# Weight loads in smaller runs and one gather moved, in a GNN layer followed by a mixture of experts

## The reference

```python
def _swiglu_ffn(x, wg, wu, wd):
    return jax.nn.silu(x @ wg) * (x @ wu) @ wd

x = x + _L0_gnn_ref(_layernorm(x, axis=-1), edge_index, ...)
h = _layernorm(x, axis=-1)
for e in range(2):
    shared = shared + _swiglu_ffn(h, sWg[e], sWu[e], sWd[e])
top_w, top_i = jax.lax.top_k(jax.nn.softmax(h @ Wr), 6)
for e in range(64):
    routed = routed + _swiglu_ffn(h, Wg[e], Wu[e], Wd[e]) * gate[:, e:e + 1]
x = x + (shared + routed + h)
```

## Time and profile before

| | us |
|---|---|
| median of three runs | 765.91 (764.79 to 767.23) |
| the profiled execution | 770.06 |
| its span, first to last instruction | 768.3 |
| PE busy | 706.6 (92%) |
| ACT busy | 215.8 |
| POOL busy | 174.6 |
| load queue (q1): data, share of the DMA engines' time | 211.33 MB, 71.8% |
| gather and scatter queue (q0) | 20.56 MB, 11.5% |

### The profile page before, as it was taken

The page is one execution under the profiler, slowest core; times in us unless marked ns, Lnnn a source line. Parts: engine busy times, 40 slices in busy tenths (PEclk is TensorE's granted clock), DMA queues, the critical chain, the costliest instruction groups (busy, mean ns, idle before and its releaser), DMA issues. The chain is left out here.

```text
span 768.3 us, 17261 instructions
## 1 busy us (share of the span) xinstructions
PE 706.6 (92%) x6966; PEld 476.9 (62%) x6966; DVE 254.0 (33%) x794; ACT 215.8 (28%) x526; POOL 174.6 (23%) x157
## 2 busy tenths in 40 slices
PE   2679999889999999999999999999999978999981
PEld 2567776657776666556566666665667756777650
DVE  6965635965121442222222112122233212221000
ACT  4732412402332222212222222221222321333330
POOL 4000000011222222332223223222333223332122
PEclk9999999999999999999999999999999998999996
DMA  8915022326999999999999999999999999999941
GB/s 285 410 55 219 24 86 104 127 87 225 359 356 347 387 375 390 387 393 386 380 377 392 378 390 375 389 386 385 386 381 371 367 339 363 372 372 373 373 127 23
DMA packets 57263, 236.32 MB, mean 308 GB/s; under 512 B 6171, under 2 KB 6335, under 8 KB 40286
## 3 DMA queue, kind: packets, MB, share of 16 engines
q1 hardware_dynamic: 46004, 211.33, 71.8%
q0 software_dynamic: 10144, 20.56, 11.5%
q10 hardware_dynamic: 1034, 3.30, 1.1%
HBM read 222.32 MB, written 12.83 MB: 306 GB/s over the span
## 5 line engine op out<-in xcount | busy, mean ns | idle before, releaser
L453 POOL DMA_INDIRECT out<-ysb,idx_sb x64 | 92.6, 1447 | 260.4 <-issue 198.3
L1445 PE MATMUL ps<-ring,xT 128*64 128x256 f32 x1296 | 148.3, 380 | 0.8 <-DMA ring<-in_L_ffn_Wu 0.8
L441 POOL DMA_INDIRECT xg<-x_tab,idx_sb x64 | 71.1, 1111 | 317.4 <-DVE idx_sb L1002 223.4
L995 DVE TENSOR_REDUCE gates<-ps 128x1 f32<-128x3 f32 (+1 forms) x62 | 10.0, 162 | 344.5 <-PE ps L1353 332.3
L1445 PEld LDWEIGHTS ps<-ring,xT 128*64 128x64 f32 x1296 | 93.2, 137 | 48.2 <-issue 2.4
L660 ACT ACTIVATE ysb<-ps 64x256 f32<-64x256 f32 x64 | 24.1, 377 | 225.0 <-PE ps L1445 150.1
L1445 PE MATMUL ps<-ring,hTj 128*64 128x256 f32 x624 | 77.1, 390 | 0.0
L1445 PE MATMUL ps<-w,xT 128*64 128x256 f32 x608 | 69.9, 379 | 0.0
L963 DVE TENSOR_TENSOR onehot<-iotaAB,slotv 125x640 bf16<-125x640 f32 (+1 forms) x64 | 67.3, 1051 | 1.3 <-PE ps L1361 0.8
L1445 PEld LDWEIGHTS ps<-ring,hTj 128*64 128x64 f32 x624 | 41.9, 138 | 29.6 <-issue 12.8
L1445 PEld LDWEIGHTS ps<-w,xT 128*64 128x64 f32 x608 | 44.1, 137 | 21.7 <-issue 0.4
(11 more groups left out here) (245 smaller groups left out, 823.9 us busy)
## 6 DMA issues: line engine op xcount, KB each, us to landing
ring<-in_L_ffn_Wg SPq DMA_DIRECT2D x41, 1024.0 KB
ring<-in_L_ffn_Wu SPq DMA_DIRECT2D x40, 1024.0 KB
ring<-in_L_ffn_Wd SPq DMA_DIRECT2D x39, 1024.0 KB
w<-in_L_ffn_Wd SPq DMA_DIRECT2D x20, 1024.0 KB
w<-in_L_ffn_Wg SPq DMA_DIRECT2D x19, 1024.0 KB
w<-in_L_ffn_Wu SPq DMA_DIRECT2D x19, 1024.0 KB
ring_x<-in_L_ffn_Wu SPq DMA_DIRECT2D x5, 1024.0 KB
ring_x<-in_L_ffn_Wd SPq DMA_DIRECT2D x5, 1024.0 KB
```

What stands on the lines that cost most here:

```text
L441: g.indirect_dma_start(out=xg[j % NX][0:ROWS[j], :], out_offset=None, in_=x_tab, in_offset=bass.IndirectOffsetOnAxis(ap=idx_sb[0:ROWS[j], ...
L453: g.indirect_dma_start(out=out, out_offset=bass.IndirectOffsetOnAxis(ap=idx_sb[0:ROWS[j], j:j + 1].bitcast(u32), axis=0), in_=ysb[j % NY][ ...
L1445: last = t_.matmul(ps[h * BIG:(h + 1) * BIG, bank, 0:AW], big(k), w[:, k, h * AW:(h + 1) * AW], start=(k == 0), stop=(k == KD - 1))
```

## The change

Gate and up weights of positions 44 to 63 are no longer loaded by one DMA each but by four, one for each of the four k slices of the tile. Each of them moves 256 KB in runs of 2 KB, and all four count on the slot's semaphore; `uses` and `landed` count accordingly. On POOL gather 53 moves from behind the base's dense transfer to a place between scatter 47 and that transfer.

```diff
@@ -310,13 +310,20 @@
-        uses = [len(range(s, len(items), NR)) for s in range(NR)]
+        PARTED, PIECES = 44, 4
+
+        def pieces(i):
+            r, j = items[i]
+            return PIECES if r < 2 and j >= PARTED else 1
+
+        uses = [sum(pieces(i) for i in range(s, len(items), NR)) for s in range(NR)]
 
         def landed(r, j):
-            return 16 * (item_of[r, j] // NR + 1)
+            i = item_of[r, j]
+            return 16 * sum(pieces(a) for a in range(i % NR, i + 1, NR))
 
@@ -373,7 +380,10 @@
                 else:
-                    sp.dma_start(ring[i % NR][:], experts[r][number[j]]).then_inc(s_ring[i % NR], 16)
+                    n = KD // pieces(i)
+                    for k in range(0, KD, n):
+                        sp.dma_start(ring[i % NR][:, k:k + n, :],
+                                     experts[r][number[j]][:, k:k + n, :]).then_inc(s_ring[i % NR], 16)
 
@@ -464,13 +474,14 @@
             for j in range(E + LAG):
-                if j < E and j <= BASE_AFTER + LAG + 1:
+                if j < E and j <= BASE_AFTER + LAG:
                     gather(j)
                 if j >= LAG:
                     if BASE_AFTER + LAG + 1 < j + 1 < E:
                         gather(j + 1)
                     scatter(j - LAG)
                 if j == BASE_AFTER + LAG:
+                    gather(j + 1)
                     add_base()
```

## The result

On 20 runs of each, measured beside each other, the changed kernel took 771.86 us (766.93 to 773.44) and the kernel before 768.05: a ratio of 1.0036, with an interval of 1.0022 to 1.0051. It is slower by a third of a per cent, and the interval is all on that side (the ratio is not that of the two medians, which would be 1.0050). Its profiled span is 770.2 us against 768.3, 1.9 more. The forecast was 768.0 on a median of 765.91, a ratio of 1.0027, with a span of 769.9. Over 20 runs the kernel before has a median of 768.05, 2.1 above the three runs that the forecast stood on; so the time itself came out 3.9 us above the forecast, and it is the ratio that can be compared.

What follows compares the result with a forecast made beforehand. PE, scatter chain and loads ran within 4% of each other, the scatter chain setting the end. Scatter 57 at 720.9 plus 49.0 gave span 769.9 against 768.3; taking 2.1 more on median 765.91 gave 768.0 us, range 760.5 to 774.5.

Steps and rivals of the forecast that it cites:

- The likeliest case: Whole kernel: scatter chain gains, then loses in the tail; 768.0 us, within 766 to 770, chance 0.38.
- The price of the 2 KB runs: Load queue: 0.20 us more a matrix, 8 us over 40, so loads drain at about 747 instead of 739.
- rival 2: Load queue: 2 KB runs cost 0.28 us or more a matrix, drain at 750; 770 to 776 us, chance 0.22.
- PE at position 60: PE late in the kernel: 6.8 us of load price against 6.3 slack makes it 0.5 us late, say 1.
- The gather: POOL: gather 53 goes by 613, base keeps 616; PE's 6.18 us wait goes, PE gains at most 4.5, the end nothing.
- The base: Dense transfer after scatter 47: some 2.5 us of 19 shorter, landing at 632, scatter 48 at 633.5.
- the turn of the packets: DMA engines: queues alternate one packet for one, so a 2 KB row waits for one load packet, now 2 KB instead of 8.
- The scatter interval of 8.4: Scatters beside loads: 1.3 us off an interval of 9.7; the chain catches up with PE by position 52.
- The tail: Scatter 57 to the end of the span: 49.0 us instead of 44.6, since loads drain at 747.
- Rival 1: Scatters beside loads: whole wait in the load queue shrinks, interval about 6.4 us; 759 to 764.5 us, chance 0.30.
- Rival 3: Whole kernel: loads eat PE's gain and the scatter chain keeps its pace; no change, 766 us, chance 0.10.
- SP's 120 issues at nothing: SP: 120 more DMAs, at most 3.4 us a position against 9.4, hidden by the full queue, cost nothing.

Runs made afterwards that it cites:

- e12: The changed kernel unaltered, measured again on the chip of e9 to e11: 770.19 us, 1.0027 of the kernel before.
- e1: The kernel before with only gather 53 moved in front of the base, all loads in their old runs: 767.42 us, 0.9999.
- e2: The changed kernel with gather 53 put back behind the base, 2 KB runs kept: 770.11 us, 1.0025 of the kernel before.
- e11: The changed kernel with 4 KB runs (two transfers a matrix) and gather 53 back behind the base: 764.52 us, 0.9951 of the kernel before.
- e5: The changed kernel with 2 KB runs only for gate and up of positions 52 to 59, gather moved: 766.96 us, 0.9993 of the kernel before.
- e7: The changed kernel with two transfers a matrix in 4 KB runs instead of four in 2 KB: 764.39 us, 0.9928 of the kernel before.
- e8: The kernel before, SP issuing each weight from position 44 on only once the third matrix back has landed: 765.94 us, 0.9974.
- e3: The changed kernel loading one slice of four for gate and up of positions 61 to 63 (weights partly wrong): 763.93 us, 0.9944 of the kernel before.
- e10: e7 with its 4 KB runs from position 24 on (80 matrices): 768.28 us, 0.9997 of the kernel before.
- e9: e7 with SP issuing each weight from position 44 on only once the third matrix back has landed: 769.09 us, 1.0018 of the kernel before.
- e6: The changed kernel with 2 KB runs from position 24 on, 80 matrices instead of 40: 776.92 us, 1.0095 of the kernel before.

## Why the prediction was right, point by point

*The sign and the size.* 1.0027 was forecast and 1.0036 (1.0022 to 1.0051) measured; the span grew by 1.9 us where 1.6 was computed. The likeliest case was the one that came. That the spans agree to 0.3 us is luck in part: they are single executions, and twelve runs of one kernel lie 5 to 10 us apart.

*The price of the 2 KB runs*, 0.20 us a matrix: the last load ends 9.2 us later, 0.23 for each of 40, and 15.3 us later with 80, 0.19 each. The drain at 747 was measured at 747.2. What the DMA engines pay is more. The load queue takes 3.35 us a matrix from 656 to 716 where it took 3.14, which is 0.31 for each matrix in small runs (0.24 in e12, which moves 19.04 MB there), and the packets' durations give 0.28. That the drain moved by less fits SP's queue: in the kernel before SP waited 7.1 us between 590 and 740 for PE to free a slot, in the changed kernel not at all. The prediction had SP at a full queue only, without that slack. So its 0.20, from the pair of windows with nothing else in them, hit the drain with a price of the engines that was too low, and rival 2, from 0.28 on, had nearly the right price and the wrong drain, 750. By the prediction's own terms the price at which PE falls behind is 6.3 / 34 = 0.19 and not 0.16.

*PE at position 60* was to be 0.5 to 1 us late and is 0.8. The short waits for weights stood at 51 and 52, within the 47 to 53 that the prediction named.

*The gather.* It went by 613 in the forecast and at 613.71 in the trace, and the base kept its place (615.30). That this part gives the end nothing is shown by e1 and, from the other side, by e2 and e11. That was forecast rightly, but the step "this part alone gives PE at most 4.5 us" was too kind, and so was "it would land by about 637, and PE needs it after 640": in e1 gather 54 landed at 639.9 and PE waited 4.43 us for it and 10.27 for ACT. The prediction looked only at the loads for what is late next. The chain from the base over scatter 48, ACT's y copy and `hTj` to PE, which stood in the earlier trace rows, was nearer.

*The base.* 2.5 of 19 us less was forecast; from its issue to scatter 48 it is 17.8 us (615.30 to 633.06) against 20.1, 2.4 less. The way to it was not the one computed: between 625 and 632 the load queue moved 633 packets while the other moved 428, and not one for one, so that the near agreement in size is not a proof of the turn of the packets.

*The scatter interval of 8.4.* Right as a price, wrong as a forecast of what the changed kernel would show: its intervals from 48 on are 10.75, 9.50, 9.30, 9.52, 9.47. The prediction let the chain catch up with PE by position 52; it had caught up at scatter 49. The timeline of all engines of the changed kernel, index and gather of two positions:

```profile
640.92 0.16 DVE L1013 TENSOR_REDUCE idx_sb<-ps 32x1 int32<-32x2 f32 x1
641.94 1.56 POOL L451 DMA_INDIRECT xg<-x_tab,idx_sb  x1 [7.37 <-DVE idx_sb L1013]
```

```profile
650.32 0.16 DVE L1013 TENSOR_REDUCE idx_sb<-ps 32x1 int32<-32x2 f32 x1
651.34 1.67 POOL L451 DMA_INDIRECT xg<-x_tab,idx_sb  x1 [6.09 <-DMA out<-ysb,idx_sb]
```

Both gathers are issued 1.02 us after the index of their position, and scatter 49, for one, follows the first at 643.81, as it stands behind it in POOL's order. So both were released by the index, which comes from PE's loop, although the profile puts the second wait down to a landing: a scatter happened to land just then, and the gather doesn't wait for scatters. That is the condition the prediction named (POOL issues scatter j-5 behind gather j+1), three positions early. ACT's y copies wait for PE only between 650 and 720 (20.9 us in seven; before, 40.0 us in seven for scatters), as forecast. Where the chain is the last, in e5 and e7, the intervals are 8.50, 8.23, 8.73 and 8.42, 8.18, 9.22, in the mean 8.5 and 8.6. That is 1.1 to 1.2 us under 9.7, near the 1.3 forecast; but e1, which has the moved gather as they have and runs of 8 KB, is at 9.15, and against it only 0.5 to 0.7 us is the runs'. And e8 reached 7.70 with runs of 8 KB. The 1.3 us was about right as a number; that the turn of the packets brings it is not shown.

*Scatter 57* was forecast at 720.9 and went at 720.77.

*The tail.* 49.0 us was forecast as 9.4, 8.2, 7.6, 4.9, 6.8, 4.8, 7.3; it was 49.4 as 9.51, 8.84, 8.60, 4.64, 6.01, 4.74, 7.09. The second and third were forecast 0.6 and 1.0 too short, the fourth to seventh 1.3 too long together, so the sum agrees by luck. I had the intervals shrink over two of them as the queue runs dry, from the 6.59 of before; but only the one in which the loads end can be shorter, and it lasts until 2 us behind their end. Here they ended 8.1 us into it, and it was a full one.

*The rivals.* Rival 1 fell by the 8.2 to 8.7 us of e5 where it needed 6.4, and e3 by its cause: what shortens an interval to 4.7 us is that the load queue is empty, not that its packets are small. Rival 3 is not it either, since e2 and e12 lie above 1.

*SP's 120 issues at nothing.* That holds: the load queue's share of the engines is no lower than before (88.6% against 88.0%), as it would be if SP issued too late.

The Trainium skill asks for at least 1 MiB per DMA for the highest bandwidth (DMA: Bandwidth & Descriptors, Rules for kernel authors). The runs bear this out only in part: 512 KB pieces lost nothing clear with many queued ahead (e7 20.34 MB, e10 19.80, against 20.01) and lost 8% with three matrices queued (e9), and 256 KB pieces lost 6% even with the full queue (18.78 against 20.01). The packets' durations put that 6% down to the 2 KB runs and not to the size of the pieces.

*Where a scatter's time goes beside loads.* The prediction left 3.6 of the 4.9 us between a loaded and an idle interval without a cause. The trace of the kernel before tells where they lie. DMA view of it from the issue of scatter 57 (723.75) to 728.4, then 728.4 to 730.8; last 742.0 to 743.7, for scatter 59, issued at 740.06 with the loads over (nothing moves from 740.06 to 742.0):

```profile
q0 software_dynamic: 8, 0.00, 0.2%
```

```profile
q0 software_dynamic: 91, 0.16, 37.0%
```

```profile
q0 software_dynamic: 96, 0.16, 80.3%
```

Beside loads, which then hold 99.5% of the engines, the first of the 80 rows moves 4.7 us after the issue, without loads 2.0; the rows then take 2.4 against 1.6 us. From the landing to the next issue on POOL it is 2.1 against 0.8, but 2.1 stands between scatters 57 and 58 in every kernel, and between 61 and 62 too, where no loads run, so it is not the loads'. So the largest part for this scatter, 2.7 us, passes before any row moves, and the stretch of the rows, which the prediction had the small packets shorten by 0.8 us, is only 0.8 us longer than without loads. In the changed kernel (scatter 58) the first row moves after 4.1 us and the rows take 3.2: smaller load packets did not shorten their stretch there.

What stays open: what a scatter waits for in those 2.7 us (the 7.70 us in e8, with three matrices queued, hint at what is queued ahead, but they are one interval); and how much of the shorter intervals in e5 and e7 is the runs' and how much the gather's.

## What to carry to other kernels

When a resource is shared by a chain of small transfers and a stream of large ones, smaller runs in the stream can help the chain and cost the stream: look for the run length at which the cost is not yet seen (here 4 KB, 0.5 to 0.7% faster over 40 matrices, nothing over 80) rather than the smallest. A wait on the busiest engine is worth nothing as long as the end belongs to a chain elsewhere; ask what ends last, and what decides how long its last links are (here, when the loads end). And a releaser in the profile is the last event before the instruction, not always its cause: a constant distance to another event (1.02 us behind the index) tells more.

## What the runs showed of the hardware that I had not expected

- A weight load split into four transfers of 32 partitions with 8 KB runs takes 37% off the load rate, 4.19 against 6.62 MB in 20 us at the same share of the engines, a packet taking 327 instead of 166 ns. The Trainium skill (DMA: Bandwidth & Descriptors, Rules for kernel authors) advises one transfer over 128 partitions rather than two halves, since the halves serialize. The measured loss is far more than the absence of a gain.
- The price of short runs goes with the packet and not with the DMA: 2 KB packets take 90 ns from DMAs of 256 KB (e6) and 92 ns from DMAs of 1 MB (the kernel before), 4 KB ones 168 ns (e7), 8 KB ones 332 ns.
- Load packets of 2 KB beside the base's rows no longer go one for one: 633 to 428 in 7 us, where it was 384 to 382. The turn-and-turn that the prediction took from that row holds for its mix of packets only.
- The scatter that is under way when the load queue runs empty holds up the next until about 2 us behind the end of the loads (4.5 us into the interval gave 6.6 us in the kernel before, 6.0 gave 7.8 in e10); the following intervals are 4.7 us. The size of the load packets moves an interval by far less, from 9.15 (e1) or 9.7 us (the kernel before) with 8 KB runs to 8.2 to 9.2 where the chain was last in e5 and e7.
- Three matrices queued are enough for the full load rate with 8 KB runs (e8, 20.20 MB in 60 us) and not with 4 KB runs (e9, 18.77; 20.34 in e7 with the full queue).
